# Weight-split subtraction moved wholly to GpSimd, and the Silu of each selection stage issued one stage later

## The reference, cut to what matters

```python
x = L0_attn_x                       # (8, 2048, 1024)
xn = _layernorm(x, axis=-1)
# recurrent half: proj = xn @ w_in.T -> gate, xa ; causal conv of width 4 ; xc @ w_gates.T
#   alpha = exp(-8*softplus(forget_base)*sigmoid(forget)) ; beta = sqrt(1-alpha**2+1e-6)
#   h[t] = alpha[t]*h[t-1] + beta*sigmoid(inp)*xc ; s = (gelu(gate)*h) @ w_out.T
# selecting half (here the forward value):
logits = (xn @ sel_w.T + sel_b).reshape(b, s, o, 8)
mask   = one_hot(argmax(logits, -1), 8)
comp   = xn @ comp_w[n].T + comp_b[n]          # n = 0..7
g      = silu(sum_n comp[n] * mask[n])
return x + s * g
```

## Time and profile before

| what | us |
|---|---|
| median of the timed runs (2) | 4925.37 |
| lowest, highest of them | 4841.22, 5009.52 |
| the profiled execution's own time | 4615.04 |
| its span on the slowest core (core 1) | 4613.5 |
| spans of the eight cores | 4575.5 to 4613.5 |
| mean granted TensorE clock of the cores | 0.898 to 0.906 |

### The profile page before, as it was taken

One profiled execution on the slowest core, in us unless ns is written; L12 is line 12 of the kernel. 1 busy time (PEld: TensorE's weight loads), 2 busy tenths in 40 slices (PEclk: granted clock), 3 DMA queues, 4 the chain that ended last, 5 costly groups with the idle time before them and its releaser, 6 DMA issues.

```text
span 4613.5 us, 46557 instructions; the slowest of 8 cores (4575.5 to 4613.5 us)
## 1 busy us (share of the span) xinstructions
PE 3723.5 (81%) x16272; PEld 1625.7 (35%) x16272; DVE 1627.8 (35%) x1968; ACT 1201.5 (26%) x1427; POOL 772.0 (17%) x448
## 2 busy tenths in 40 slices
PE   3988998896398799989639889988964988998995
PEld 1433443342133344434213334433422433443442
DVE  2333334333333433433233343343333334334333
ACT  2342221222134322122213432212221342222221
POOL 1211111111111111111111111111111111111111
PEclk8987999998699899999869889999987988999998
DMA  2322332332222223233222223323312222222321
GB/s 70 95 73 75 90 92 83 91 86 61 73 92 73 83 92 92 83 91 85 62 73 92 81 75 91 92 82 92 92 55 82 92 73 82 92 92 74 96 89 63
DMA packets 362776, 380.61 MB, mean 83 GB/s; under 512 B 12304, under 2 KB 356384, under 8 KB 362544
## 3 DMA queue, kind: packets, MB, share of 16 engines
q1 hardware_dynamic: 354816, 352.36, 25.9%
q0 software_dynamic: 7728, 25.27, 1.9%
HBM read 369.20 MB, written 8.39 MB: 82 GB/s over the span
## 4 chain that ended last, share of the span: by engine, by line
PE 55%; DVE 22%; ACT 9%; issue 5%; DMA 4%; POOL 3%; DVEq 1%; ACTq 0%; POOLq 0%
PE pg L272 54%; DVE mxb L86 5%; DVE msk L86 4%; ACT wh L86 4%; DVE accb L86 4%; DMA poolA<-xT 3%; DVE poolC L86 3%; POOL wl L86 2%; DVE poolB L86 1%; ACT sf L86 1%; DVE wl L86 1%; DVE si L86 1%; DMA hb<-xT 1%; ACT scr L86 1%; DVE scr L86 1%
## 5 line engine op out<-in xcount | busy, mean ns | idle before, releaser
L272 PE MATMUL pg<-xnh,wh 128*128 128x512 bf16 x4608 | 1803.3, 391 | 621.6 <-POOL wl L86 468.7
L272 PE MATMUL pg<-xnl,wh 128*128 128x512 bf16 x4608 | 1801.4, 391 | 0.0
L272 PE MATMUL pg<-xnh,wl 128*128 128x512 bf16 x4608 | 1797.1, 390 | 0.0
L86 POOL TENSOR_TENSOR wl<-w,wh 128x1024 bf16<-128x1024 f32 x336 | 718.5, 2138 | 3650.5 <-ACT wh L86 3592.4
L86 DVE TENSOR_TENSOR wl<-w,wh 128x1024 bf16<-128x1024 f32 x336 | 412.6, 1228 | 2023.0 <-ACT wh L86 2017.3
L86 ACT ACTIVATE wh<-w 128x1024 bf16<-128x1024 f32 x672 | 710.1, 1057 | 1491.9 <-PE pg L272 1450.7
L272 PEld LDWEIGHTS pg<-xnh,wh 128*128 128x128 bf16 x4608 | 461.6, 100 | 1221.3 <-issue 724.2
L272 PEld LDWEIGHTS pg<-xnh,wl 128*128 128x128 bf16 x4608 | 462.3, 100 | 580.5 <-issue 78.8
L272 PEld LDWEIGHTS pg<-xnl,wh 128*128 128x128 bf16 x4608 | 460.9, 100 | 568.5 <-issue 69.5
L272 PE MATMUL pg<-xch,wh 128*128 128x512 bf16 x768 | 298.2, 388 | 101.5 <-POOL wl L86 101.5
L272 PE MATMUL pg<-xcl,wh 128*128 128x512 bf16 x768 | 297.7, 388 | 0.0
(11 more groups left out here) (59 smaller groups left out, 939.9 us busy)
## 6 DMA issues: line engine op xcount, KB each, us to landing
w<-selT SPq DMA_DIRECT2D x256, 512.0 KB, 5.0
w<-cmpT SPq DMA_DIRECT2D x256, 512.0 KB, 5.5
w<-w1T SPq DMA_DIRECT2D x64, 512.0 KB, 5.5
w<-w2T SPq DMA_DIRECT2D x64, 512.0 KB, 4.8
w<-w3T SPq DMA_DIRECT2D x32, 512.0 KB, 5.0
hb<-xT POOLq DMA_DIRECT2D x32, 256.0 KB, 9.1
poolA<-xT POOLq DMA_DIRECT2D x32, 256.0 KB, 4.0
outT<-poolC POOLq DMA_DIRECT2D x32, 256.0 KB, 2.6
```

What stands on the lines that cost most here:

```text
L86: return fn(*a, **k)
L272: last = tensor.matmul(bank[:, :], wop[:, wcol:wcol + P], xop[:, k * TT:(k + 1) * TT], start=(idx == 0), stop=(idx == 23))
```

## The change

The `wl` subtraction of piece 0 moves from VectorE to GpSimd, which now makes both pieces. The Silu of stage i is emitted behind the component groups of stage i+1 instead of at the end of stage i (that of stage 7 stays at the end, behind that of stage 6). Since `accb` has one buffer, its next writer now waits for the Silu that reads it (`acc_guard`).

```diff
-                    eng, engn, semn = ((vector, "ve", "ve") if pc == 0
-                                       else (gpsimd, "gp", "gpc"))
+                    eng, engn, semn = (gpsimd, "gp", "gpc")
...
+                def emit_silu(ii):
+                    c.needt(scalar, "sc", acc_toks[ii])
+                    c.need(scalar, "sc", "ve", free_hb[ii][1])
+                    ins = scalar.activation(
+                        gg[:, ii * TT:(ii + 1) * TT], accb[:, :], AF.Silu)
+                    silu_toks[ii] = ("sc", c.inc(ins, "sc"))
+
+                acc_toks = [None] * KC
...
                     if i == 7 and t + 1 < nt:
                         xn_rdy_box[0] = emit_LN(t + 1)
+                    if i > 0:
+                        emit_silu(i - 1)
                     c.needt(vector, "ve", L_toks[7])
...
+                    acc_guard = silu_toks[i - 1] if i > 0 else prev_silu_tile[0]
+                    if acc_guard is not None:
+                        c.needt(vector, "ve", acc_guard)
                     ins = vector.tensor_copy(accb[:, :], si[:, 7 * TT:8 * TT])
...
-                    c.need(scalar, "sc", "ve", tok[1])
-                    c.need(scalar, "sc", "ve", free_hb[i][1])
-                    ins = scalar.activation(
-                        gg[:, i * TT:(i + 1) * TT], accb[:, :], AF.Silu)
-                    silu_toks[i] = ("sc", c.inc(ins, "sc"))
+                    acc_toks[i] = ("ve", tok[1])
+                    if i == 7:
+                        emit_silu(7)
+                        prev_silu_tile[0] = silu_toks[7]
```

More of the change, by code:

```diff
@@ L183, in build @@
         half_seq = [0]
+        prev_silu = [None]
+        prev_silu_tile = [None]
         @block.vector
```

## The result

| | before | changed |
|---|---|---|
| ratio of the times, with its 95% interval | 1 | 0.925 (0.9209 to 0.929) |
| median of the timed runs | 4844.7 us (10) | 4475.0 us (11) |
| lowest timed run | 4606.5 us | 4260.8 us |
| profiled execution, own time | 4615.0 us | 4266.2 us |
| its span on the slowest core | 4613.5 us | 4264.6 us (core 3) |

The changed kernel is 7.5% faster. In part of the executions of every kernel here, the cores of one die (or of both) hold a lower granted clock, which is what parts the medians from the lowest runs: a ratio leaves such runs out, is not given where too few others are left, and where a profile has such cores I read another core of it.

A forecast was written before the change was run, and what follows sets the result against it. TensorE bounds the kernel, with a 12.6 us stall at 28 boundaries: 4613.5 - 353 - 5 + 13 + 14 - 8 - 4 = 4270 us of span. A 0.80 clock in 57% of the work raised it to 4680, range 4270 to 4930.

The forecast's parts named there:

- Silu one stage later, with `wl` on GpSimd: At 28 selection-stage boundaries: third half ready at 19.7 us, before TensorE needs it at 20.7; gain 28 x 12.6 = 353 us.
- Recurrence: In stage 0, `scr` is held longer by GpSimd's two subtractions: 0.85 us for each of 4 splits in 4 tiles, 14 us.
- Convolution: Small `xa` copy runs ahead of the subtractions, later `poolC` instructions meet the second one: -0.5 us, 16 times, -8 us.
- Table: Behind the layer norm, the first Silu loads the table while VectorE is busy: -1.3 us three times, -4 us.
- Loads and start: Second `wl` piece 1.1 us later behind stage 0's recurrence, before final and layer norm loads, at the start: 13 us.
- Sum against the profiled execution: Whole kernel: all gains and costs taken from 4613.5 give 4270 us of span, 4272 with 1.5 around it, 7.4% less.
- From there to the timed runs: Whole kernel: clock 0.80 explains the median's 310 us above the profile; 57% of the way from 4270 to 5015, forecast 4680.
- the quiet case: Lower end of the forecast range, 4270 us: the span summed from the profiled execution, without the 0.80 clock term.
- No turn: At stage boundaries, GpSimd gets no turn inside the selection chain; 8.7 us of waiting stays, time 4890; chance 0.10.
- Cover missed: At 28 boundaries, the half comes after TensorE's ready groups end, at 23 to 24 us; time 4760; chance 0.09.
- A denser TensorE loses its clock: In the seven stages, unbroken work lowers the clock to 0.80, 18 us a stage; throughout, 5015 us; chance 0.07.
- The Silu was not what held TensorE: At stage boundaries, the Silu's wait is not what stops TensorE, so little changes; chance called small.

The follow-up runs named there:

- e3: Changed kernel with the `wl` subtraction of piece 1 made twice, three GpSimd subtractions a half; profiled execution 4432.2 us.
- e1: Changed kernel with piece 0 of `wl` back on VectorE, Silu still later; no ratio, core 6 spans 4558.2 us against 4596.4 for the kernel before.

## Why the prediction was right in its mechanism and wrong in its size

*The bound.* Right: TensorE and one stall a boundary, and it is gone. The prediction parts its 12.6 us into 10.3 of standing still and 2.3 of clock; its own times give 30.5 - 20.7 = 9.8, and the list of waits 10.2. The 12.6 comes from the period and does not hang on it.

*Silu one stage later, with `wl` on GpSimd.* Right, nearly to the figure: first mask done at 12.0 (12.0 measured by the copy's start), GpSimd asking at 14.25 (14.1), half ready at 19.7 (19.0), cover 1.0 us (1.7), chain over at 33 (31.1), period 82.9 (82.9). One size was off: a subtraction inside the chain delays VectorE by 1.7 us (seven `mxb` take 9.40 instead of 5.88 us with two among them), not by 2.1. With 2.1 for each of two, the laid out times would put the maximum at 11.7 and not at the 11.2 written. The open question, whether GpSimd gets a turn inside a running chain, went as chosen: it lost 0.5 us in two turns, and e3 confirms it by overrunning the cover. From a tile's first component of stage 0 to that of stage 7, the four tiles together take 352 us less on core 3 and 354 on core 5, for 353 forecast.

*Recurrence.* Right: 14 us forecast, 14.0 measured (342.6 - 328.6 us, core 3 against core 1). *Convolution.* -8 forecast. From the first to the last `xa` copy, the three tiles that have them take 158.5 us (core 3) where the kernel before took 168.9 (core 1): -10. *Table.* Behind the next tile's layer norm the load now stands ahead of the first of the two Silus and no longer behind the wait for `accb`, as forecast; its worth was not measured alone. *Loads and start.* Not separated.

*Sum against the profiled execution.* 4272 us forecast, 4266.2 measured. That the two are 6 us apart is in part luck: core 1 was the slowest before and core 3 after, and core by core the span falls by 322 to 361 us, 337 on average, where the sum has 343. The boundaries are in it as forecast; where the spread between the cores comes from is not shown.

*From there to the timed runs.* This is the step that failed. I took the median of two timed runs, 4925 us, as the kernel's time, explained its distance to the profile by a clock of 0.80 in 57% of the work, and laid the same share on the changed kernel. That gave 4680, 5.0% less than 4925, and 3.4% less than the 4844.7 that more runs of the same kernel give. The runs showed that the share is no property of the kernel: the kernel before also ran in 4606.5 us and the changed one in 4260.8, 4260.8 and 4265.4, each where its profiled execution was (4615.0 and 4266.2). So the term, some 410 us on top of 4270, has to be nothing on that footing, and the ratio is 0.925, where the sum's own 7.4% stood ready. I had the right number and diluted it. The range, 4270 to 4930, holds the median of the changed kernel, 4475, but its lower end lies above the lowest runs, for the same reason: I let the quiet case be the edge of the range instead of its middle.

*The rivals.* No turn: refuted by the 4.86 us of GpSimd's pair inside the chain. Cover missed: it was not, but e3 shows that one more subtraction is enough for it. A denser TensorE loses its clock: in the profiled execution the rows of 1460 to 1660 us show 1.00 on all of it, on each of the eight cores, and over the whole span the mean clock of the cores is 0.928 to 0.931, up from 0.898 to 0.906; a share of 88% at 0.80 is not there. The Trainium skill (TensorE: Matmul & The Clock Gate, Part 1) tells of a limiter that takes a die to 13/16 once three of its cores run dense matmuls and holds it there while they do; these 200 us, dense on all eight cores at 1.00, do not agree with it. The Silu was not what held TensorE: half true, and I had not seen that half. Behind the Silu stood a second wait of nearly the same length, that of `wl` piece 0 for the chain on VectorE, which only e1 makes visible.

## What to carry to other kernels

When a wait goes, write down what stands next in each engine's order and when it would be ready; here two waits lay one behind the other, and of the 12.6 us that both parts of the change save together, one alone saved 1.6 and the other alone lost 0.4. Where two engines shut each other out, count every instruction of both that falls inside the chain, also those that the change moves into it. And when the timed runs of a kernel scatter by several per cent while its profile sits at their lower end, forecast the ratio from the profile's own time, and do not carry the scatter of two runs over to the new kernel.

## What the runs showed of the hardware that was not expected

- A stop of TensorE of 3.0 us left the granted clock at 1.00 (e3: 47 matmuls in the next 10 us); one of 10.3 us brought it to 0.79 in the next 10 us (37 matmuls). In these rows the second price of a stop comes only with the long one.
- GpSimd and VectorE take turns instruction by instruction even in a dense chain: a pair of 128x1024 subtractions took 4.86 us inside the chain and 4.39 us outside it, while the VectorE instructions that met one counted about 2.4 us for 0.75. The pair outside:

```profile
1500.47 4.39 POOL L86 TENSOR_TENSOR wl<-w,wh 128x1024 bf16<-128x1024 f32 x2 [5.68 <-ACT wh L86]
```

  So GpSimd lost 0.5 us a pair and VectorE 3.5 (9.40 instead of 5.88 us for seven `mxb`): here the price fell on the engine with the short instructions. The Trainium skill (SBUF — State Buffer, section "SBUF: two separate sides") says that whoever starts first keeps the port for the whole instruction; the trace agrees, since a mask that starts beside a subtraction ends only 0.5 to 0.6 us behind it.
